# Attention and expert block on one core: where half of each even key block's weighted sum is issued

## What is computed

```python
qkv = x @ Wqkv.T + bqkv
qkv = qkv.reshape(B, H, S, 3 * hd)          # a plain reshape: head h takes rows 64h..64h+63
q, k, v = jnp.split(qkv, 3, axis=-1)
scores = jnp.einsum('bhsd,bhtd->bhst', q, k) * (1.0 / math.sqrt(hd))
attn = jax.nn.softmax(scores, axis=-1)
vals = jnp.einsum('bhst,bhtd->bhsd', attn, v)
```

## Time and profile before

| | |
|---|---|
| median of three executions | 556.86 us (556.68 to 558.76) |
| the profiled execution | 557.98 us, span 556.1 us |
| PE busy | 519.1 us, 93% of the span |
| ACT busy | 494.8 us, 89% |
| DVE busy | 362.8 us, 65% |
| POOL busy | 219.2 us, 39% |
| TensorE clock granted | 0.99 of full speed over the span |

### The profile page before, as it was taken

How to read it: one execution, slowest core, us unless ns; L and a number is a source line. 1 busy time by engine, 2 the same in 40 slices (tenths; PEclk the granted TensorE clock), 3 DMA queues, 4 the chain that set the end, 5 groups by cost and what they waited for, 6 DMA issues and landing times. The chain is left out here.

```text
span 556.1 us, 14357 instructions
## 1 busy us (share of the span) xinstructions
PE 519.1 (93%) x4064; PEld 215.3 (39%) x4064; DVE 362.8 (65%) x1271; ACT 494.8 (89%) x571; POOL 219.2 (39%) x429
## 2 busy tenths in 40 slices
PE   7488889999999999999999999999999999999983
PEld 6233333334343434343433333343434343433352
DVE  4435457677867666677767667677676666664466
ACT  1279989999999999999999999999999999998962
POOL 1223233344443334444443343444433344443335
PEclk9999999999999999999999999999999999999997
DMA  4573333333333333333333333333333332333010
GB/s 100 128 199 90 89 96 78 77 97 88 89 90 89 96 98 84 76 78 93 88 90 90 98 93 83 72 88 91 88 89 95 98 86 65 91 96 84 17 32 14
DMA packets 85497, 48.44 MB, mean 87 GB/s; under 512 B 61508, under 2 KB 76240, under 8 KB 85456
## 3 DMA queue, kind: packets, MB, share of 16 engines
q1 hardware_dynamic: 70162, 43.07, 30.0%
q10 hardware_dynamic: 15294, 4.82, 3.8%
HBM read 32.91 MB, written 14.94 MB: 86 GB/s over the span
## 5 line engine op out<-in xcount | busy, mean ns | idle before, releaser
L547 ACT ACTIVATE probs<-ps_scores 128x1024 f32<-128x1024 f32 x512 | 485.8, 1028 | 42.9 <-DMA q_scr<-qk_parts 19.6
L735 PE MATMUL ps_attn<-probs,values 128*32 128x512 f32 x2048 | 248.1, 599 | 0.4 <-issue 0.4
L717 PE MATMUL ps_scores<-query_stack,key_stack 32*128 32x512 f32 x1024 | 130.7, 500 | 17.5 <-ACT probs L547 11.4
L717 PEld LDWEIGHTS ps_scores<-query_stack,key_stack 32*128 32x128 f32 x1024 | 49.4, 183 | 167.9 <-ACT probs L547 164.1
L422 POOL TENSOR_SCALAR var_eps<-moments 128x1 f32<-128x1 f32 x64 | 12.3, 192 | 222.7 <-DVE moments L1078 149.5
L735 PEld LDWEIGHTS ps_attn<-probs,values 128*32 128x32 f32 x2048 | 54.0, 109 | 110.5 <-issue 110.3
L765 PE MATMUL ps_side<-experts_gated,h2T 128*128 (+1 forms) x228 | 74.7, 409 | 0.0
L1067 DVE RECIPROCAL sums_inv<-sums 128x128 f32<-128x128 f32 x32 | 30.5, 952 | 32.5 <-DMA attnT<-a_scr 32.5
L1074 DVE TENSOR_TENSOR x<-ps_side,x_gated 128x128 f32<-128x128 f32 x31 | 9.0, 292 | 60.8 <-PE ps_side L765 57.2
L1150 DVE TENSOR_TENSOR weighted<-ps_side,coef 128x256 f32<-128x256 f32 x114 | 46.5, 408 | 2.4 <-PE ps_side L765 2.4
L471 POOL TENSOR_TENSOR mix<-weighted 128x512 f32<-128x512 f32 x31 | 39.7, 1280 | 0.0
(11 more groups left out here) (129 smaller groups left out, 498.9 us busy)
## 6 DMA issues: line engine op xcount, KB each, us to landing
key_stack<-k_scr SPq DMA_DIRECT2D x128, 128.0 KB, 2.7
query_stack<-q_scr SPq DMA_DIRECT2D x121, 64.0 KB, 2.2
q_scr<-qk_parts SPq DMA_DIRECT2D x188, 32.0 KB, 2.0
k_scr<-qk_parts SPq DMA_DIRECT2D x64, 64.0 KB, 1.7
a_scr<-attn ACTq DMA_DIRECT2D x126, 18.0 KB
sums<-a_scr SPq DMA_DIRECT2D x32, 64.0 KB, 2.1
attnT<-a_scr SPq DMA_DIRECT2D x32, 64.0 KB, 2.2
out_dram<-out_all ACTq DMA_DIRECT2D x29, 64.0 KB, 1.8
```

Of the source, the lines that this page charges most:

```text
L547: nc.scalar.activation(probs[:, k % RING, g, :], ps_scores[:, slot(k, g), :], ACT.Exp, scale=SCALE)\
L717: mm = nc.tensor.matmul(out_, key_stack[p0:p0 + 32, parity, 2 * k:2 * k + 2, :].rearrange("p j r -> p (j r)"), query_stack[p0:p0 + 32, par ...
L735: mm = nc.tensor.matmul(ps_attn[q:q + 32, :], values[:, parity, g, k, :], probs[:, k % RING, g, h * HALF:(h + 1) * HALF], start=(k == 0), ...
```

## The change

`weigh` gets a range of columns of `ps_attn`. The sums of the even key block of each pair, 512 columns, are issued in two halves: columns 0 to 255 right behind the side products (ahead of the branch on `flag`), columns 256 to 511 where all 512 stood before, behind the scores of the odd block. The sums of the odd key block stay whole and where they were. Waits for `attn_saved`, `values_done` and `probs_ready` stand on the first half, `pv_done` is raised by the second. `start` is set on the first half of block 0 alone. Nothing else is changed, and no other engine's program.

```diff
--- before.py
+++ after.py
@@ -723,19 +723,22 @@
                     if exact or h == 1:
                         mm.then_inc(scores_ready[k][g], 1)
 
-            def weigh(t, t1, parity, k):
-
-                if k == 0:
-                    reached(pe, ev["attn_saved"], t)
-                    reached(pe, ev["values_done"], t1)
+            def weigh(t, t1, parity, k, columns=slice(0, HALF)):
+
+                if columns.start == 0:
+                    if k == 0:
+                        reached(pe, ev["attn_saved"], t)
+                        reached(pe, ev["values_done"], t1)
+                    for g in range(G):
+                        reached(pe, probs_ready[k][g], t1)
                 for g in range(G):
-                    reached(pe, probs_ready[k][g], t1)
                     for h in range(2):
                         q = 32 * (2 * g + h)
-                        mm = nc.tensor.matmul(ps_attn[q:q + 32, :], values[:, parity, g, k, :],
-                                              probs[:, k % RING, g, h * HALF:(h + 1) * HALF],
-                                              start=(k == 0), stop=(k == KT - 1), tile_position=(0, q))
-                mm.then_inc(pv_done[k], 1)
+                        mm = nc.tensor.matmul(ps_attn[q:q + 32, columns], values[:, parity, g, k, :],
+                                              probs[:, k % RING, g, h * HALF + columns.start:h * HALF + columns.stop],
+                                              start=(k == 0 and columns.start == 0), stop=(k == KT - 1), tile_position=(0, q))
+                if columns.stop == HALF:
+                    mm.then_inc(pv_done[k], 1)
 
 
             def c_project(ps, y1, b):
@@ -849,14 +852,18 @@
                 batch = {n: batch_of(pe, at[-n]) for n in (2, 3, 4) if n <= before}
                 return at, batch
 
+            def weigh_past(at, parity, before, k, columns):
+
+                if k >= 0:
+                    weigh(at[0], at[1], parity, k, columns)
+                elif before:
+                    weigh(at[-1], at[0], 1 - parity, KT + k, columns)
+
             def between_sides(at, parity, before, k, exact):
 
                 scores(at[0], at[1], parity, k, exact)
-                for past_k in (k - 3, k - 2):
-                    if past_k >= 0:
-                        weigh(at[0], at[1], parity, past_k)
-                    elif before:
-                        weigh(at[-1], at[0], 1 - parity, KT + past_k)
+                weigh_past(at, parity, before, k - 3, slice(HALF // 2, HALF))
+                weigh_past(at, parity, before, k - 2, slice(0, HALF))
                 if k + 1 < KT:
                     scores(at[0], at[1], parity, k + 1, exact)
 
@@ -891,6 +898,7 @@
                     if k == 6:
                         drained2(at, before, after, 0)
                         side3(ps_side, at, batch, parity, before, after, 0)
+                    weigh_past(at, parity, before, k - 2, slice(0, HALF // 2))
                     with pe.If(flag == 0):
                         between_sides(at, parity, before, k + 1, True)
                     with pe.Else():
```

## The result

The changed kernel takes 563.64 us (median of six executions, 561.78 to 565.09) against 556.77 (556.59 to 559.08) for the one before, run alongside: 1.011 times, with an interval of 1.0084 to 1.0137. That is slower by 6.9 us, inside the range given and more than the 2.4 us forecast. The profiled execution took 563.94 us with a span of 562.1, so the spans differ by 6.0.

What follows compares the result with a forecast made beforehand. PE was taken to bound the steady tiles, with 0.30 us idle in each; +6.5 (steady tiles), -3.7 (sixteen pairs), -0.4 (end) and 0.1 off for pauses made +2.4, forecast 559.2 us, range 549.5 to 565.

Steps and rivals of the forecast that it cites:

- The price of the switch: Each pair of blocks: one more array switch 0.10, costlier sums-to-scores 0.02, split run 0.02; 0.14 us of PE per pair.
- the 0.30 that I had counted: Idle PE in a steady tile of 15.76 us, waiting for exponentials: 0.21 us at k = 0, 0.09 at k = 4.
- The first and last tiles: Sixteen pairs with few side products fall from 3.91 us to ACT's 3.68: -0.23 each, -3.7 us.
- The end: Last two blocks' sums have 0.43 us less in front of them, half of block 4 being done earlier: -0.4 us.
- Waits: Check of semaphores, queues and other engines: nothing later, 0.8 us margin for the copy before block 0's first half.
- O to E: Stretch from odd block's scores to the next even block's: 2.30 us, PE the limit, to get 0.43 shorter.
- price in the steady tiles: Tiles 4 to 29: 0.56 us added less 0.30 idle filled, about +0.25 us per tile, +6.5 us.
- pauses in unrolled parts: PE's pauses in the program's unrolled parts: 0.1 us taken off, 1 or 2 us either way with a longer program.
- The hidden switch: Rival: half sums' first load goes in during the expert product, 0.04 us per pair, 549 us; chance 0.18.
- the half passes too short for their loads: Rival: uncovered loads or switch cost 0.1 us in each of a pair's two runs, +23 us, 580 us; chance 0.14.
- The late copy: Rival: DVE's copy over 0.8 us later is paid in each tile; 0.3 would give +9, 568 us; chance 0.06.
- the second rival: Half passes too short to hide loads or switch: 580 us in full, a quarter 565; chance 0.14.

Runs made afterwards that it cites:

- e1: Changed kernel's cut into two halves, but both left behind the odd block's scores, against the kernel before: 564.04 us, ratio 1.0115.
- e4: Only 64 of the 512 columns go ahead, 448 stay behind the scores, against the kernel before: 562.41 us, ratio 1.0103.
- e7: Changed kernel with PE's exact path, flag load and flag branches left out: 554.77 us, ratio 0.9964 to the kernel before.
- e8: Kernel before the change with PE's exact path, flag load and flag branches left out: 553.84 us, ratio 0.9953 to the kernel before.
- e2: Changed kernel with the half ahead at k = 0, 2 and 4 only, not at k = 6: 559.97 us, ratio 1.0041 to the kernel before.
- f1: Half ahead only in tiles 0 to 3 (not at k = 6) and the last two tiles, against the kernel before: 560.46 us, ratio 1.0073.
- f3: f2 with PE's exact path and flag branches left out: 549.47 us, ratio 0.9849 to the kernel before.
- e9: Kernel before with one more product per product of scores in PE's exact path, never executed: 557.99 us, ratio 1.0005.
- f2: As f1, with the half also ahead at k = 0 in every tile, against the kernel before: 555.8 us, ratio 0.9966.
- e5: All 512 columns of the even block's sum ahead of the odd block's scores: 581.69 us in one run, kernel before 556.89.

## Why the forecast was near in range and short in size

**The price of the switch: right.** Pairs of 3.83, 4.14, 3.94 and 4.02 us stand against 3.84 (3.91 - 0.21 + 0.14), 4.14, 3.95 and 4.09 by the steps. e1 (cut, not moved: nothing) and e4 (an eighth moved: the same price) show that it hangs on the switch. The Trainium skill (TensorEngine Tiling (Array Packing), key properties) says that a change of tiling mode drains the engine; the measured distance of 0.30 from expert pass to half round, against a pass of 0.215, agrees and puts 0.09 us on it. The one pair that is off is k = 6, by 0.07. Before, PE stood there in front of the `squares` product a little longer (L752 at 307.54 and L671 at 307.74, against 310.07 and 310.21 after), so the tile held some 0.06 more idle time than the 0.30 that I had counted. e7's tile of 15.93 is the forecast's 16.0 less this.

**The first and last tiles: right in kind, near in size.** Without the branches, e7 less e8, they give -2.0 and -1.1 us, 3.1 together against -3.7, and the pairs of tile 2 in e7 that wait for ACT take 3.67 us as forecast. That the change itself shows -2.7 and -1.1, 3.8 together, is partly luck with the pauses: in these tiles the kernel before takes 3.6 us more than e8, and the changed one 2.8 more than e7. One of these pauses; PE after, in tile 2:

```profile
58.73 0.51 PE L717 MATMUL ps_scores<-query_stack,key_stack 32*128 32x512 f32 x4 [1.49 <-issue]
```

Where the earlier trace rows has a wait of 0.63 for ACT at this place, there are 1.49 us of waiting for PE's sequencer.

**The end: wrong, small.** -0.4 gave 0. The sums behind the last scores start 0.44 after them and end in 3.42 us instead of 3.57, but the last of them wait for the last exponential. PE after, at the end:

```profile
539.15 1.06 PE L737 MATMUL ps_attn<-probs,values 128*32 128x512 f32 x8
```

The exponential before it began at 537.86 and took 1.14, till 539.00. I had counted PE's queue only and not who releases its last item.

**The step that failed** is the one headed Waits. It went through semaphores, DMA queues and other engines, and found nothing later. It left out the queue that the change shortens the cover of: PE's own instruction stream. I had taken O to E as a stretch where "PE is the limit", and it was, but with 0.1 us to spare over the branch chain hidden behind it. Cutting the stretch by 0.43 laid 0.30 bare, with 0.08 more at the first side product: 0.39 us for two tiles (16.03 + 16.22 less twice 15.93), 4.7 us over 24 tiles. It was in no rival either. The net price of a steady tile, with the further idle time in front of `squares`, came to 0.17 and not 0.25, and this hides part of the miss. Summed for the spans:

| term | forecast us | measured us | by |
|---|---|---|---|
| price in the steady tiles | +6.5 | +4.2 | e7 less e8 |
| loop top | none | +4.7 | tiles after, less e7's |
| first and last tiles | -3.7 | -3.1 | e7 less e8 |
| end | -0.4 | 0 | last exponential to end |
| pauses in unrolled parts | -0.1, 2 either way | +0.1 | +0.8 left of +9.7, -0.7 left of -3.8 |

These make +5.9, and the spans differ by 6.0.

**The rivals.** The hidden switch fell: the distance from expert pass to half round is 0.30, not 0.22. So did the half passes too short for their loads: the second half round starts 0.24 us after the first, which is the 0.215 of a half and the 0.02 that the sum had for the first round of a run, and the pairs aren't longer than forecast.

```profile
299.19 0.40 PE L737 MATMUL ps_attn<-probs,values 128*32 128x256 f32 x4
```

The late copy held up a weight load once in the whole run, by 0.3 us. The time of 563.6 lies near "a quarter of the second rival", the upper bound of the range, and that is chance: its mechanism is absent, and the term that fills its place had no part in the range.

**The long branches.** They took up to 4.0 us in e1, 2.7 in the changed kernel and 0.98 in the kernel before (profiled runs), and moved the totals of e1, e2 and f1 by several us. That they vanish with the branches is shown by e7, e8 and f3, and that more code jumped over doesn't add to the total by e9. What they wait for can be read from the traces, though no run was made for it: blocks of the program itself that are being loaded. The pages count these transfers (number and MB) on queue q8; before, after, e7 and e8:

```profile
q8 instruction: 26, 0.43, 0.3%
...
q8 instruction: 29, 0.48, 0.4%
...
q8 instruction: 13, 0.21, 0.2%
...
q8 instruction: 10, 0.16, 0.1%
```

Each is 16 KB, and in the changed kernel none starts between 115 and 475 us, while the loop repeats. The long branch of its tile 2 is this one:

```profile
L902 PEldq COMPARE_BRANCH  x1: 2695/2695/2695, 56.0 to 56.0; - x1
```

A block began to load at 55.77 us, and the branch ended at 58.67. In e1 it is 473.08 and 475.66 (the branch above). All 32 flag branches of over 0.5 us in the fourteen traces end 2.3 to 3.0 us after the start of such a load. So a branch is long when it comes while the code is being loaded, and how long depends on how far the load has got; an edit that shifts the two against each other moves the pauses. **Still open** is whether the load that goes with a long branch is always one that the branch itself asks for, and how the loads could be kept out of its way.

## What to carry to other kernels

When a stretch of an engine's queue is shortened, ask not only which semaphores end in it but what its sequencer does meanwhile: a loop branch, a value load and a branch took 1.6 us here, and a stretch of 2.29 us hid them with 0.1 to spare. Splitting work to fill idle time costs a switch of the array each time (0.1 us here, 0.14 with the split run), so do it only at the places whose idle time is larger, as f2 and f3 do. Judge such a change by the period of a steady tile beside the median, since pauses in code that runs once can move the total by more than the change does.

## What the runs showed of the hardware, unexpected

- PE's sequencer began the loop branch with 20 weight loads and passes still to start (the changed kernel) and with 24 (e5), with different queues in front of it; so work behind a branch can be late although PE has been busy all along.
- One COMPARE_BRANCH on PE takes 0.207 us in the loop and took 2.7 to 4.0 us at single places passed once, with PE standing idle up to 2.8 us behind it (e1, until 40.76 us); each such branch ended 2.3 to 3.0 us after a 16 KB block of the program had begun to load. Leaving the flag's load, branches and other path out gave the kernel before 3.0 us (553.84 against 556.89).
- Cutting a 512-column product into two of 256, with twice the loads, cost at most 0.03 us per tile for 16 products (e1: 15.78 against 15.75).
